# FP4 stages of a transformer kernel: each group's inner values quantised in their own turn, three of four quantiser products on VectorE

## The reference, cut to what matters

```python
BLOCK = 16
_GRID = [0.0, 0.5, 1.0, 1.5, 2.0, 3.0, 4.0, 6.0]
_MID = [0.25, 0.75, 1.25, 1.75, 2.5, 3.5, 5.0]

def fp4_quant_dequant(x):            # along the last dim
    xb = x.reshape(shape[:-1] + (shape[-1] // BLOCK, BLOCK))
    scale = jnp.max(jnp.abs(xb), axis=-1, keepdims=True) / 6.0
    scale = jnp.maximum(scale, jnp.float32(1e-12))
    xn = xb / scale
    idx = jnp.searchsorted(_MID, jnp.abs(xn))
    q = _GRID[idx] * jnp.sign(xn) * scale
    return q.reshape(shape)

def fp4_linear(x, w):
    return jnp.einsum('bsk,nk->bsn', fp4_quant_dequant(x), fp4_quant_dequant(w))
```

## Time and profile before

| | us |
|---|---|
| median of 3 runs | 1977.69 |
| lowest, highest | 1976.85, 1982.12 |
| the profiled execution | 1977.81 |
| its span, first to last instruction | 1976.0 |

### The profile page before, as it was taken

One profiled execution on the slowest core, in us unless ns is written; L12 is line 12 of the kernel. 1 busy time (PEld: TensorE's weight loads), 2 busy tenths in 40 slices (PEclk: granted clock), 3 DMA queues, 4 the chain that ended last, 5 costly groups with the idle time before them and its releaser, 6 DMA issues.

```text
span 1976.0 us, 30933 instructions
## 1 busy us (share of the span) xinstructions
PE 1694.2 (86%) x10673; PEld 964.4 (49%) x10673; DVE 1488.1 (75%) x2485; ACT 946.8 (48%) x1791; POOL 405.0 (20%) x722
## 2 busy tenths in 40 slices
PE   5799999548999999999998889999967678885675
PEld 4688888301111111111112578888835545553454
DVE  5855555679999999999993665556779758885884
ACT  3223322606888888888887522332244311111552
POOL 5310010400000010000002310010145632333442
PEclk9899999858999999999999999999978779997777
DMA  3000000210010101100110010000000000000000
GB/s 119 1 0 0 0 0 1 99 62 18 29 31 21 34 23 35 36 20 21 34 28 7 6 49 0 0 0 0 1 1 0 0 1 2 0 1 1 1 21 22
DMA packets 25292, 35.77 MB, mean 18 GB/s; under 512 B 5808, under 2 KB 19696, under 8 KB 24672
## 3 DMA queue, kind: packets, MB, share of 16 engines
q1 hardware_dynamic: 25184, 34.38, 5.8%
HBM read 22.57 MB, written 8.78 MB: 16 GB/s over the span
## 4 chain that ended last, share of the span: by engine, by line
PE 66%; DVE 19%; ACT 5%; issue 5%; POOL 3%; DMA 2%; SPq 1%; DVEq 0%; POOLq 0%; ACTq 0%
PE PS L909 12%; PE PS L420 11%; PE PS L897 9%; PE PS L409 6%; PE PS L410 6%; PE PS L411 6%; PE PS L886 5%; DVE neg_half L1025 4%; DVE shared L1705 3%; ACT probs L974 3%; DVE qk_all L1240 3%; PE PS L1458 2%; PE PS L1570 2%; DVE qk_all L1243 1%; PE PS L1472 1%
## 5 line engine op out<-in xcount | busy, mean ns | idle before, releaser
L1025 DVE TENSOR_REDUCE neg_half<-PS 128x2 f32<-128x1024 f32 x512 | 600.8, 1219 | 43.7 <-PE PS L886 28.6
L974 ACT ACTIVATE probs<-PS 128x512 f32<-128x512 f32 x1024 | 529.0, 604 | 169.7 <-PE PS L897 169.6
L491 ACT ACTIVATE shared<-PS 128x512 f32<-128x512 f32 x256 | 152.6, 597 | 398.0 <-PE PS L411 384.3
L897 PE MATMUL PS<-qk_all 51*128 51x512 bf16 x1024 | 278.2, 387 | 16.9 <-ACT probs L974 12.1
L559 DVE TENSOR_TENSOR shared<-shared,PS 128x512 f32<-128x512 f32 x256 | 174.2, 685 | 153.2 <-ACT shared L491 151.8
L909 PE MATMUL PS<-probs,Vg 128*32 128x512 f32 x2048 | 274.8, 609 | 0.1
L420 PEld LDWEIGHTS PS<-wd,shared 128*128 128x128 f32 x2048 | 248.7, 192 | 10.7
L420 PE MATMUL PS<-wd,shared 128*128 128x128 f32 x2048 | 250.0, 275 | 0.0
L886 PE MATMUL PS<-qk_all 48*128 48x512 bf16 x1024 | 201.2, 403 | 45.0 <-DVE neg_half L1025 23.5
L897 PEld LDWEIGHTS PS<-qk_all 51*128 51x128 bf16 x1024 | 71.6, 93 | 335.9 <-ACT probs L974 319.1
L567 DVE SCALAR_TENSOR_TENSOR x<-PS,gates,x 128x128 f32 (+1 forms) x512 | 144.1, 344 | 69.1 <-PE PS L420 69.1
(11 more groups left out here) (203 smaller groups left out, 2295.9 us busy)
## 6 DMA issues: line engine op xcount, KB each, us to landing
split<-shared SPq DMA_DIRECT2D x16, 384.0 KB, 3.3
qk_all<-split SPq DMA_DIRECT2D x64, 96.0 KB
qk_all<-split SPq DMA_DIRECT2D x64, 64.0 KB
qk_all<-split SPq DMA_DIRECT2D x64, 32.0 KB
shared<-OTs SPq DMA_DIRECT2D x60, 32.0 KB
probs<-in_ret_const SPq DMA_DIRECT2D x1, 1538.5 KB, 6.6
qk_all<-negT SPq DMA_DIRECT2D x96, 4.0 KB, 1.8
SC<-inverse SPq DMA_DIRECT2D x3, 512.0 KB, 5.1
```

What stands on the lines that cost most here:

```text
L491: act.activation(sg[:, f, :], bank(f), ACT.Silu).then_inc(s["silu"], 1)
L897: pe.matmul(bank(RING_AT + use % RING), qs[rows, slot, 1, pair, kt * P:(kt + 1) * P], qs[rows, slot, 0, pair, half * GW:(half + 1) * GW], ...
L974: act.activation(probs[:, n % 2, STRIPS * strip + pair, :], bank(RING_AT + use % RING), ACT.Exp, scale=ATT_SCALE).then_inc(s["exped"], 1)
L1025: dve.tensor_reduce(neg_half[m % 2][:, i % 2, :, at], bank(use_bank(i, m), 2).rearrange("p (s w) -> p s w", s=STRIPS), AX.X, ALU.max, nega ...
```

## The change

Both FP4 stages get another order and another split of work:

- The inner values of group g are quantised wholly in turn g (`ffn_hidden`, then `ffn_hidden_round`), right behind the four silu products of that group, which now stand together (`products`).
- The tokens are quantised two groups ahead (g + 2) instead of one; group 1's are prepared before turn 0.
- DVE does three of the four multiplications of the quantisers: both of the inner values and the first of the tokens. POOL keeps the second of the tokens (`ffn_scale`).
- Everything is written out, without the loop. The PSUM pairs rotate through all groups (`ffn_slot`), the transposed tokens use bank 6 instead of 7, the inner chunks alternate between banks 6 and 7, and `down` of group g - 1 runs in turn g.

The core of the diff (the rest follows from it):

```diff
+        def q_exponents(dve, link, src, code, step, amax, scale, nb, done):
+
+            link(dve.tensor_reduce(amax, q_blocks(src), AX.X, ALU.max, apply_absolute_value=True))
+            yield
+            link(dve.tensor_scalar(scale, amax, 1.0 / 6.0, 1e-12, ALU.mult, ALU.max))
+            link(dve.reciprocal(amax, scale))
+            yield
+            link(dve.tensor_scalar(amax, amax, DOWN, None, ALU.mult))
+            link(dve.tensor_tensor(q_blocks(code), q_blocks(src), q_wide(amax, nb), ALU.mult))
+            yield
+            dve.tensor_scalar(step.bitcast(I32), code.bitcast(I32), EXPONENT, None, ALU.bitwise_and).then_inc(done, 1)
...
+        def ffn_tokens(dve, link, n, g):
+
+            c = done_groups(n) + g
+            dve.wait_ge(ffn["xn"], c + 1)
+            wait(dve, ffn["xq"], c)
+            yield from q_exponents(dve, link, fxn, tcode, tstep, tmax, tscale, GT * NB_C, ffn["t_exp"])
+            yield
...
+        def ffn_hidden_round(dve, link, n, g):
+
+            c = done_groups(n) + g
+            dve.wait_ge(ffn["h_step"], c + 1)
+            q_round(dve, link, hcode, hstep).then_inc(ffn["h_code"], 1)
+            dve.wait_ge(ffn["h_code"], c + 1)
+            wait(dve, ffn["hT_ps"], 3 * c)
+            dve.tensor_tensor(q_blocks(hq), q_blocks(hcode), q_wide(fscale, GT * NB_I), ALU.mult).then_inc(ffn["hq"], 1)
...
+        def ffn_slot(n, g, j):
+            return (GT * (done_groups(n) + g) + j) % 3
...
+            ffn_tokens_round(dve, link, n, 0)
+            for _ in ffn_tokens(dve, link, n, 1):
+                pass
+            ffn_tokens_round(dve, link, n, 1)
+            for g in range(GROUPS):
+                products(g)
                 dve.wait_ge(s["h"], (c0 + g + 1) * GT)
-                q_measure(dve, link, uq, c0 + g)
...
+                ffn_hidden(dve, link, n, g)
+                if g + 2 < GROUPS:
+                    for _ in ffn_tokens(dve, link, n, g + 2):
+                        pass
+                ffn_hidden_round(dve, link, n, g)
+                if g > 0:
+                    add(g - 1)
+                if n == 3 and g > 1:
+                    dve.wait_ge(s["added"], c0 + g - 1)
+                    ln_stats(dve, g - 2)
+                if g + 2 < GROUPS:
+                    ffn_tokens_round(dve, link, n, g + 2)
...
+        def ffn_scale(pool, n, g):
+            s = ffn
+            c = done_groups(n) + g
+            pool.wait_ge(s["t_code"], c + 1)
+            wait(pool, s["xT_ps"], c)
+            pool.tensor_tensor(q_blocks(xq), q_blocks(tcode), q_wide(tscale, GT * NB_C), ALU.mult).then_inc(s["xq"], 1)
...
+            ffn_tokens_step(act, n, 0)
+            ffn_normalise(act, n, 1)
+            ffn_tokens_step(act, n, 1)
+            tokensT(0)
...
+            silu(0, (0, 1, 2))
+            ffn_normalise(act, n, 2)
+            for g in range(GROUPS):
+                silu(g, (3,))
+                if g > 0:
+                    for c in range(len(CHUNKS)):
+                        hiddenT(g - 1, c)
+                if g + 1 < GROUPS:
                     tokensT(g + 1)
...
+                ffn_hidden_step(act, n, g)
+                if g + 2 < GROUPS:
+                    ffn_tokens_step(act, n, g + 2)
+                if g + 1 < GROUPS:
+                    silu(g + 1, (0, 1, 2))
+                if g + 3 < GROUPS:
+                    ffn_normalise(act, n, g + 3)
...
+            def gate_up(g, js):
+                for j in js:
+                    u = ffn_slot(n, g, j)
+                    pe.wait_ge(s["xT"], c0 + g + 1)
+                    wait(pe, s["h"], (c0 + g) * GT + j - 2)
...
+            tokens(0)
+            gate_up(0, (0, 1, 2))
+            for g in range(GROUPS):
+                gate_up(g, (3,))
+                if g > 0:
+                    for c in range(len(CHUNKS)):
+                        hiddenT(g - 1, c)
+                if g + 1 < GROUPS:
+                    tokens(g + 1)
+                if g > 0:
+                    down(g - 1)
+                if g + 1 < GROUPS:
+                    gate_up(g + 1, (0, 1, 2))
```

More of the change, by code:

```diff
@@ L1196, in fp4_weights_pe @@
             last.then_inc(s["t_ps"], 1)
[L1206 to L1209 removed]
+        EXPONENT = 0x7F800000
         def q_blocks(v):
             return v.rearrange("p (n k) -> p n k", k=FB)
[L1214 to L1215 removed]
@@ L1217, in q_measure @@
[L1217 to L1251, removed]
@@ L1431, in ffn_act @@
-            q_rounding_step(act, tq, c0)
-            ffn_normalise(act, n, 1)
-            tokensT(0)
-            act.activation(fsg[:, 0, 0:1], ident[:, 0:1], ACT.Silu).then_inc(s["silu0"], 1)
-            act.wait_ge(s["silu0"], c0 // GROUPS + 1)
-            peeled(act, turn)
-            q_rounding_step(act, uq, c0 + GROUPS - 1)
+                    wait(act, s["h"], (c0 + g) * GT + j - 2)
+                    act.activation(fsg[:, u, :], bank(2 * u)[:, 0:INNER], ACT.Silu).then_inc(s["silu"], 1)
@@ L1447, in tokens @@
                 pe.wait_ge(s["xq"], c0 + g + 1)
-                wait(pe, s["added"], c0 + g - 2)
-                wait(pe, s["hT"], 3 * (c0 + g - 2))
+                wait(pe, s["hT"], 3 * (c0 + max(g - 1, 0)))
                 for j in range(GT):
-                    last = pe.transpose(bank(7)[:, j * P:(j + 1) * P], xq[:, j * P:(j + 1) * P], ident[:, :])
+                    last = pe.transpose(bank(6)[:, j * P:(j + 1) * P], xq[:, j * P:(j + 1) * P], ident[:, :])
                 last.then_inc(s["xT_ps"], 1)
-            def gate_up(g, j):
-                pe.wait_ge(s["xT"], c0 + g + 1)
-                wait(pe, s["h"], (c0 + g) * GT + max(j - 2, 0))
-                for half in range(2):
-                    last = pe.matmul(bank(2 * (j % 3) + half)[:, 0:INNER], xqT[:, j * P:(j + 1) * P],
-                                     wguT[:, half * INNER:(half + 1) * INNER], start=True, stop=True)
-                last.then_inc(s["gu"], 1)
@@ L1462, in hiddenT @@
-            def hiddenT(r, c, tokens_before):
+            def gate_up(g, js):
+                for j in js:
+                    u = ffn_slot(n, g, j)
+                    pe.wait_ge(s["xT"], c0 + g + 1)
+                    wait(pe, s["h"], (c0 + g) * GT + j - 2)
+                    for half in range(2):
+                        last = pe.matmul(bank(2 * u + half)[:, 0:INNER], xqT[:, j * P:(j + 1) * P],
+                                         wguT[:, half * INNER:(half + 1) * INNER], start=True, stop=True)
+                    last.then_inc(s["gu"], 1)
```

182 lines of the change are left out of this document (53 added, 129 removed).

## The result

The changed kernel is slower: 1998.38 us median of 5 runs (1992.59 to 2003.92) against 1977.69 us of the kernel before on the same chip. The ratio is 1.0093, 95% interval 1.0076 to 1.0111. The profiled execution took 2000.7 us, its span is 1998.9 us.

A forecast was written before the change was run, and what follows sets the result against it. DVE was taken to set the pace. First stage +8.9, its fill +2.7, second stage +11.2, its fill +1.5, overlaps -1.5, on 1977.8 us gave about 2001 us; range 1985 to 2011, own forecast 1995 to 2008 (0.72).

The forecast's parts named there:

- the fourth product's wait: Before a turn's fourth silu product, DVE idles about 2.3 us for product 0, low-clock matmuls (2.81 us) and silu.
- The products' block: The four silu products at the turn's top on DVE, including the wait before the fourth: 4.41 us.
- The rest of the turn: DVE after the silu products: exponents 5.46 and 2.70, inner rounding and product 4.94, add 0.69, tokens' rounding 1.42 us.
- the overlap: Unchained neighbouring DVE instructions overlap by some 0.05 us, about 0.1 us a turn, -1.5 us in all.
- The ends: Each stage's last turns: turn 6 at 17.05 us, turn 7 with its drain at 26.2 us.
- The split: Three products added to DVE, 3.89 us a turn, against 3.0 us of lost time from POOL and a 0.83 us wait removed.
- So far the balance is about zero: DVE work per turn before counting the new order: +3.9 - 3.0 - 0.8 us.
- the drain's gain: Last inner group quantised in its own turn, no longer a turn later: some 6 us a stage.
- rival 1: PE keeps full clock at the turn's top, shrinking the wait by 1.43 us in 14 turns: 1981 us; chance 0.12.
- rival 2: The fourth product does not wait at all, products take 2.0 instead of 4.41 us: 1968 us; chance 0.04.
- rival 3: PE stays at low clock through the turn and becomes the bound, 20.5 us a turn: 2012 us; chance 0.08.
- rival 4: The remaining POOL product and the statistics still lock DVE, 1.06 us in 12 turns: 2014 us; chance 0.04.

The follow-up runs named there:

- the experiment on turn 0: Changed kernel with, on ACT in turn 0, the fourth tile's silu moved ahead of group 2's normalisation; 1995.59 us, stages' sum 349.6 instead of 352.7.
- the split alone: Kernel before, written out, old order kept, with three of the four quantiser multiplications on DVE; 1971.57 us, ratio 0.9943 to 0.9979 to the kernel before.
- the idle products: Changed kernel plus four or six unread matmuls on PE behind each turn's first three gate_up; 1989.10 us with four, 1983.48 us with six.
- with cover: Changed kernel with the tokens' exponents between the third and fourth silu product on DVE, and the add before the inner rounding; 1980.97 us.

## Why the prediction was right

1998.4 us measured, 2001 predicted, for the mechanism that was named: the fourth product's wait. Point by point:

- **The products' block.** Predicted 4.41 us; measured 1915.37 to 1919.80, 4.43. PE was idle for 6.58 us before it (5 to 6 predicted) and at 0.50.
- **The rest of the turn.** Inner exponents 5.34 (5.46), tokens' exponents 2.60 (2.70), inner rounding and product 4.86 (4.94), add and tokens' rounding 1.92 (2.11). The products of 1408 columns took 1.63 (1.60). So the turn was 19.15 instead of 19.6 and 19.92 instead of 20.4. The mis-sized term is the overlap: where an instruction is not chained to the one before, it starts 0.08 to 0.10 us before the other's end in the timeline, in five or six places a turn. I had taken 0.1 us a turn; it was about 0.45.
- **The ends.** Turn 7 with its drain, predicted 26.2 us from the products' start: 1969.93 to 1996.16 is 26.2. Turn 6, predicted 17.05: 16.86 in the second stage. Its wait for ACT's step, predicted 1.55, was 1.53.
- **Turn 0.** A miss that the total hid. The fourth silu stands behind ACT's normalisation of group 2, which I had not walked through; the experiment on turn 0 gave back 3.1 us in both stages together. To the first `gate_up` the fills grew by only 2.2 and 0.1 us, from there to product 3 by another 0.8 and 1.8.
- **The sum.** From the end of product 3 of turn 0 to the last add 156.2 us (160.1) and 152.4 (155.8). Fills +3.0 (+2.7) and +1.9 (+1.5), counted to that product. All in all the stages grew by 17.8 instead of 22.8, most of the 5 us for the overlap above. That the total still came within 3 us of the median is in part luck: the rest of the kernel happened to be slower in these runs.
- **The split.** "So far the balance is about zero" was nearly right for the turns and left out that the same edit shortens fills and drains; alone it gains 7.1 us. The forecast had put the drain's gain, 6 us a stage, down to the quantisation in the group's own turn; the split alone already gives 6.5 and 4.3 us of the 9.7 and 5.2 by which the ends are shorter.
- **The rivals.** PE at full clock (rival 1) is what the idle products made in some turns: 17.89 us, a little below the 18.2 named for it. That the product doesn't wait at all (rival 2) did not occur, but was built: with cover, turns of 17.63. PE as the bound (rival 3) fell: `down` took 2.84 us, at full clock, and PE was idle for a third of the turn. The lock by the POOL product that stays (rival 4) fell: it runs beside products with an operand in PSUM, which took 503 to 522 ns in all 64 cases, and no 512- or 32-column DVE instruction of the turns took more than 0.69. (At 2012 us rival 3 lay outside the range, too, which the recorded list of what it leaves out does not say.)

What stays open: why PE in some turns kept its clock over 3.57 us of idle time and in others had lost it after 2.46.

## What to carry to other kernels

Where one engine's queue sets the pace, count its waits, not its work: a round trip over two other engines (here product, matmul, silu, product) must have other work of its own engine between its ends, and grouping like instructions takes that work away. When a change bundles an order with a split of work, time them apart: here the split alone was worth -7 us and the order on top of it +25. Price an edit at the ends of a pipeline apart from its middle, since what is hidden in a turn is bare in a drain.

## What the runs showed of the hardware

- Beside POOL's 2.58 us product a 512-column DVE rounding took 2.69 us instead of 0.69, while an add with a PSUM operand kept its 0.69 and the statistics their 0.86. Moving a product of 1.62 us from POOL to DVE thus shortened a middle turn of the second stage by 0.36 us and lengthened one of the first, where the statistics stood in between, by 0.36.
- Behind six idle products of 512 columns PE's granted clock was 1.00 to the end of the drain, and the two stages took 3.8 and 2.9 us less: `down` took 2.94 us instead of 5.43 and 4.45. Idle work on PE made the kernel faster.
- The fourth `gate_up` at 0.50 took 2.69 us and at 1.00 took 1.42. In 13 of the changed kernel's 14 turns the clock was back before `down` (2.84 to 2.94 us); in one it came back only within it (4.04).
